# One register value per pair, masked one-hots released pair by pair, QKV two steps per group

## The reference, cut to what matters

```python
h = relu(layernorm(x)); z = ln(h, ln1_g, ln1_b)
q, k, v = (z @ W + b).reshape(512, 8, 64)            # Wq, Wk, Wv
scores = einsum('ehd,ehd->eh', q[src], k[dst]) * scale + edge_bias
p = exp(scores - segment_max(scores, src)[src])
out = segment_sum(p / segment_sum(p, src)[src] * v[dst], src)     # layer 0
# then layers 1 to 3: segment sums over the same edges between dense layers
```

## Time and profile before

| | before |
|---|---|
| three runs | 443.1, 440.94, 443.72 us; median 443.1 us |
| profiled execution | 438.14 us, its span 436.7 us |
| TensorE busy | 391.0 us, 90% |
| VectorE busy | 319.4 us, 73% |
| ScalarE busy | 166.9 us, 38% |
| first to last pair matmul | 28.09 to 141.88 us |

### The profile page before, as it was taken

One profiled execution on the slowest core, in us unless ns is written; L12 is line 12 of the kernel. 1 busy time (PEld: TensorE's weight loads), 2 busy tenths in 40 slices (PEclk: granted clock), 3 DMA queues, 4 the chain that ended last, 5 costly groups with the idle time before them and its releaser, 6 DMA issues.

```text
span 436.7 us, 5306 instructions
## 1 busy us (share of the span) xinstructions
PE 391.0 (90%) x1794; PEld 287.8 (66%) x1794; DVE 319.4 (73%) x664; ACT 166.9 (38%) x275; POOL 2.3 (1%) x14
## 2 busy tenths in 40 slices
PE   2679878779889899999898999999978999999995
PEld 1455444445545678888675878878746878877773
DVE  6788958577683588899696697868885568677436
ACT  1625534454210444235346671335244341124420
POOL 2000000000000000000000000000000000000000
PEclk9999989898899899999998999999989999999989
DMA  8405867684521430004640032320050005000002
GB/s 250 191 2 81 109 99 107 93 117 91 72 54 24 146 121 1 2 2 153 238 187 2 0 102 92 101 93 0 1 194 0 0 0 194 0 3 0 0 2 96
DMA packets 16297, 32.94 MB, mean 75 GB/s; under 512 B 1360, under 2 KB 1488, under 8 KB 16272
## 3 DMA queue, kind: packets, MB, share of 16 engines
q1 hardware_dynamic: 15744, 32.25, 29.2%
q10 hardware_dynamic: 528, 0.36, 0.4%
HBM read 21.07 MB, written 1.05 MB: 51 GB/s over the span
## 4 chain that ended last, share of the span: by engine, by line
PE 60%; DVE 21%; DMA 6%; ACT 5%; issue 4%; SPq 0%; DVEq 0%; ACTq 0%
PE acc L1253 7%; PE bank L1335 6%; DMA big<-z_sb 6%; PE bank L1236 6%; PE acc L1124 4%; PE bank L1124 4%; PE acc L1137 3%; PE acc L1138 3%; PE acc L1306 3%; PE bank L1320 3%; PE bank L1138 3%; PE bank L1137 3%; DVE wide_rounded L713 3%; DVE stats L580 2%; DVE c_rounded L719 2%
## 5 line engine op out<-in xcount | busy, mean ns | idle before, releaser
L1253 PE MATMUL acc<-wide_rounded,c_rounded 128*126 128x512 f32 x200 | 64.1, 465 | 15.4 <-issue 7.4
L1253 PEld LDWEIGHTS acc<-wide_rounded,c_rounded 128*126 128x126 f32 x200 | 37.4, 202 | 43.2 <-issue 37.9
L713 DVE TENSOR_SCALAR wide_rounded<-iota_f,picked 128x512 fp32r<-128x512 f32 x100 | 41.8, 481 | 26.3 <-PE acc L1253 25.0
L427 ACT COPY z_sb<-acc 126x512 f32<-126x512 f32 x37 | 21.7, 586 | 71.6 <-PE acc L1253 40.7
L451 ACT ACTIVATE wide<-wide,low_col 128x512 f32<-128x512 f32 x32 | 21.4, 715 | 32.3 <-DVE low_col L829 32.2
L1335 PEld LDWEIGHTS bank<-v_sb,big 128*128 128x128 f32 x256 | 29.9, 192 | 5.2 <-issue 4.8
L1335 PE MATMUL bank<-v_sb,big 128*128 128x65 f32 x256 | 31.7, 277 | 0.0
L1236 PE MATMUL bank<-t_sb,wslot 128*128 128x512 f32 x64 | 31.6, 620 | 0.0
L549 DVE TENSOR_TENSOR wslot_rounded<-wslot,wide_rounded 128x512 fp32r<-128x512 f32 x24 | 16.2, 687 | 20.9 <-ACT wslot L360 20.9
L719 DVE TENSOR_TENSOR c_rounded<-row_bc,wslot_rounded 128x1008 fp32r<-128x1008 bf16 x25 | 30.0, 1201 | 0.0
L576 DVE TENSOR_TENSOR big_rounded<-big,big_rounded 128x1024 fp32r<-128x1024 f32 x24 | 29.1, 1222 | 0.4
(11 more groups left out here) (292 smaller groups left out, 780.1 us busy)
## 6 DMA issues: line engine op xcount, KB each, us to landing
big<-z_sb SPq DMA_DIRECT2D x33, 252.0 KB
big<-in_w SPq DMA_DIRECT2D x4, 2048.0 KB, 7.9
x_sb<-in_x SPq DMA_DIRECT2D x8, 256.0 KB, 5.1
big<-in_w_3t SPq DMA_DIRECT2D x2, 1024.0 KB, 6.7
row_bc<-in_rows SPq DMA_DIRECT2D x7, 256.0 KB, 6.6
wslot<-in_wq SPq DMA_DIRECT2D x1, 1024.0 KB, 8.3
wslot<-in_wk SPq DMA_DIRECT2D x1, 1024.0 KB, 10.2
wslot<-in_wv SPq DMA_DIRECT2D x1, 1024.0 KB, 12.3
```

Source lines behind the costliest of these rows:

```text
L427: nc.scalar.copy(stage[0:BROWS, b % STAGES, :], a).then_inc(S["staged"], 1)
L713: nc.vector.tensor_scalar(hot_ring[:, u, k, :], iota_f[:, :], picked[:, 0, s0 + k:s0 + k + 1], None, ALU.is_equal)
L1253: last = nc.tensor.matmul(to, st_ring[:, u, 2 * k + a, :, :].rearrange("p w k -> p (w k)"), hot_ring[:, u, k, :], start=False, stop=False, ...
```

## The change

It has four parts. (1) `rows_u` keeps one number per pair, the block's number plus one; the wait uses it as it is, and the bank is its low two bits, so `choices` loads 8 values in place of 16, and block b goes to bank (b+1) mod 4. The matmul and the two small VectorE operations for the bank's number go. (2) The value's range is stated, so no assertion is made for the slice. (3) VectorE waits for each pair of group g-2 ahead of the one-hot that overwrites it, in place of once for the whole group. (4) `qkv_group`: two steps after each group from 3 to 15, then two after every other group from 17 to 23; before, two after odd groups and one after even ones, and four after group 23.

```diff
-ENDS, PICK, BANKS, NEEDS = 130, 200, 300, 400
-SPARE = 1
+ENDS, PICK, NEEDS = 130, 200, 400
...
-        rows_u = sb("rows_u", [1, SLOTS, 2], U16)
+        rows_u = sb("rows_u", [1, SLOTS], U16)
...
-        qkv_group = [g for g, steps in enumerate([7, 4, 3] + [2, 1] * 10 + [4]) for _ in range(steps)]
+        qkv_group = [g for g, steps in enumerate([7, 4, 3] + [2] * 13 + [0, 2, 0, 2, 0, 2, 0] + [2]) for _ in range(steps)]
...
-                a = bank[b % ACC][0:BROWS, :]
+                a = bank[(b + 1) % ACC][0:BROWS, :]
...
-            dve.wait_ge(S["tables"], 4)
-            link(nc.vector.tensor_single_scalar(bank_i[:, :], bank_i[:, :], ACC - 1, ALU.bitwise_and))
-            mark(nc.vector.tensor_scalar(bank_c[:, :], bank_i[:, :], float(N), -float(SPARE * N), ALU.mult, ALU.add))
...
-                nc.vector.tensor_single_scalar(rows_u[:, c, 0], bank[4][0:1, column(BANKS)], float(SPARE * N), ALU.add)
-                nc.vector.tensor_single_scalar(rows_u[:, c, 1], bank[4][0:1, column(NEEDS)], float(NBK + 1),
+                nc.vector.tensor_single_scalar(rows_u[:, c], bank[4][0:1, column(NEEDS)], float(NBK + 1),
                                                ALU.add).then_inc(S["rows_ready"], 1)
...
                 for k in ks:
+                    if freed is not None:
+                        dve.wait_ge(S["pair_mm"], freed + (k + 2))
                     nc.vector.tensor_scalar(hot_ring[:, u, k, :], iota_f[:, :], picked[:, 0, s0 + k:s0 + k + 1], None,
                                             ALU.is_equal)
...
-                dve.wait_ge(S["pair_mm"], (g - RING + 1) * GROUP + 1)
-                build(g, g % RING, g * GROUP)
+                build(g, g % RING, g * GROUP, (g - RING) * GROUP)
...
-                dve.wait_ge(S["pair_mm"], j * GROUP + (FIXED - GROUP + 1))
-                build(NG - 1, 0, FIXED)
+                build(NG - 1, 0, FIXED, j * GROUP + (FIXED - RING * GROUP))
...
-                nc.tensor.matmul(bank[4][0:1, column(BANKS)], bank_c[:, :], slot_hot[:, c], start=True, stop=True)
...
-                    rows_u[0:1, s0:s0 + n, :].rearrange("o s a -> o (s a)"), engines=[mybir.EngineType.PE])
+                    rows_u[0:1, s0:s0 + n], engines=[mybir.EngineType.PE], min_val=1, max_val=NBK + 1,
+                    skip_runtime_bounds_check_because="a block's number plus one, made on the chip from a table")
...
-                    to = acc[0:BROWS, bass.ds(held[2 * k], N)]
-                    pe.wait_ge(S["evacuated"], held[2 * k + 1])
+                    pe.wait_ge(S["evacuated"], held[k])
+                    to = acc[0:BROWS, bass.ds((held[k] & (ACC - 1)) * N, N)]
```

More of the change, by code:

```diff
@@ L105, in gnn_kernel @@
         ends = sb("ends", [NBK, 2])
-        bank_c = sb("bank_c", [NBK, 1])
         need_c = sb("need_c", [NBK, 1])
-        bank_i = sb("bank_i", [NBK, 1], I32)
         ends_row = sb("ends_row", [1, NBK + 3])
@@ L335, in _ @@
                            allow_small_or_imprecise_dtypes=True).then_inc(S["tables"], 2)
-            nc.gpsimd.iota(bank_i[:, :], [[0, 1]], base=0, channel_multiplier=1).then_inc(S["tables"], 1)
             nc.gpsimd.iota(need_c[:, :], [[0, 1]], base=-NBK, channel_multiplier=1,
@@ L708, in slot_columns, with one_hots @@
                 step(base + 3, slot_masks(first), False)
-            def one_hots(u, s0, ks=range(GROUP)):
+            def one_hots(u, s0, ks=range(GROUP), freed=None):
                 for k in ks:
+                    if freed is not None:
+                        dve.wait_ge(S["pair_mm"], freed + (k + 2))
                     nc.vector.tensor_scalar(hot_ring[:, u, k, :], iota_f[:, :], picked[:, 0, s0 + k:s0 + k + 1], None,
@@ L724, in left_sides, with build @@
                         [P, 2 * GROUP, BW, KW]), ALU.mult).then_inc(S["built"], 1)
-            def build(g, u, s0):
-                one_hots(u, s0)
+            def build(g, u, s0, freed=None):
+                one_hots(u, s0, freed=freed)
                 left_sides(u, s0)
@@ L1264, in _ @@
             bias_turned()
-            pe.wait_ge(S["tables"], 7)
+            pe.wait_ge(S["tables"], 6)
             pe.wait_ge(S["lows_ready"], 1)
@@ L1275, in _ @@
             for g in range(NG - 1):
-                pairs(g, g % RING, held[2 * GROUP * (g % 2):2 * GROUP * (g % 2 + 1)])
+                pairs(g, g % RING, held[GROUP * (g % 2):GROUP * (g % 2 + 1)])
                 if g == 0:
```

## The result

The changed kernel takes 422.47 us (median of 4 runs, 420.65 to 423.52) against 442.02 us beside it: **0.956, 95% interval 0.949 to 0.963**. The profiled execution took 420.65 us, its span is 419.1 us; 17.6 us of span are gone.

What follows compares the result with a forecast made beforehand. It took TensorE's sequencer to bound the kernel, with transfers already pacing the first part. Block 28's bank free at 102.7 plus 22.2 put the last pair at 124.9; 443.1 - 17.1 gave 426.0 us, range 418 to 434.

Steps and rivals of the forecast that it cites:

- The transfers set the first part's pace: Pair stage to block 28, about 103 us: transfers already set the pace, 2.35 us a block; faster TensorE gains nothing.
- The load's term: Loads of 8 values in place of 16 on TensorE's sequencer: 2.2 us each, saving 2.3 per period.
- Register work: Per pair on TensorE's sequencer: 0.40 us in place of 0.50, bounds 0.25 and 0.50; eight pairs save 0.8 us.
- The signs: What would show it: loads 1.9 to 2.4 us, last pair at 122 to 128, copies to block 28 awaiting DMA.
- the second rival: Transfers cost more than allowed, or the clock drops in their waits: gain 8 to 12, 431 to 435 us; 14%.
- QKV: From group 17 on, 8 steps left where 13 were: five steps, 4.3 us, move to where transfers set the pace.
- One-hots: VectorE's waits pair by pair ahead of its one-hots: costed at 0 to 1 us in all.
- The sum: Block 28's bank free at about 102.7 us, plus 22.2: last pair ends at 124.9 in place of 141.88.
- The 1.3 us for handing over: Added behind block 28 to the longest of four near-equal chains, 20.9 us, making 22.2.
- The slower one: Mask and product make TensorE's sequencer wait ahead of every pair: decides from 0.79 us per pair, 462 at 1.0; 3%.
- The one with a larger gain: Register work 0.25 us per pair, loads 1.92, transfers 2.1 a block: last pair about 119.5, 418 to 421; 9%.
- The one in which a load's time is not by the value: Loads on TensorE's sequencer stay near 4.4 us; gain from register work and QKV alone, 436 to 440 us; 2%.

Runs made afterwards that it cites:

- e7: The changed kernel with loads of 16 values and two slice assertions per pair, both put back: 438.84 us, 0.990 of the kernel before.
- e9: The kernel before with only the new places of the QKV steps: 438.60 us, 0.997.
- e10: The kernel before with only the one-hots released pair by pair: 440.92 us, 0.999.
- e8: The changed kernel with four stage places in place of three, so four transfers may be in flight: 418.24 us, 0.945 of the kernel before.
- e12: The changed kernel transferring only half the columns of each staged block: last block copied 89.6 us after the first pair matmul, in place of 97.0.
- e11: The kernel before transferring only half the columns of each staged block: pair stage 108.6 us in place of 113.8.
- e3: The changed kernel with the QKV steps where they were before: 425.43 us, 0.966 of the kernel before.
- e4: The changed kernel with VectorE waiting for the whole group ahead of the first one-hot, as before: 422.59 us, 0.960 of the kernel before.
- e2: The changed kernel with each load reading 16 values again, 8 of them used: 425.81 us, 0.965 of the kernel before.
- e6: The changed kernel with each pair's slice asserted twice again: 424.86 us, 0.961 of the kernel before.
- e5: The kernel before with the range of the loaded values stated, so no assertions: 428.08 us, 0.967.

## Why the prediction was right

- **The bound before.** The load was what ended the gaps that the profile put down to ScalarE or to "issue". e7 shows it: with loads and assertions as before and the rest new, gaps and period return. QKV (e9: 0.997, 0.993 to 1.000) and one-hots (e10: 0.999) alone do nothing clear to a kernel that its sequencer bounds.
- **The transfers set the first part's pace.** Block 28 moved by 0.58 us where 0.8 were forecast; e8 and e12 confirm the bound. That they set it *already before* was too strong: there both bounds lay side by side. With half the bytes, e11 gained 5.6 us in that part, of which shorter loads can be 3.2, the larger share. The prediction used this only to say that the first part would not get shorter, and that held.
- **The load's term**: 2.2 us forecast, 2.28 measured.
- **Register work** was mis-sized: 0.40 us per pair forecast, with 0.25 as the lower bound; 0.22 measured. The FUSED_REGOPS of 146 ns was gone, where I had kept one. With 0.22 and the measured loads of 2.53, 2.25, 2.68 and 1.24 us the sequencer's chain is 16.8 us (an estimate) and not the longest: TensorE's own 20.4 us is. Since the sum went by the 20.9 of the sequencer, this cost it 0.5 us. That so large a miss cost so little is owed to a second chain of nearly the same length, not to the register term.
- **The signs.** Most came as named, but one did not: the prediction called its size wrong if copies of blocks 29 to 35 waited for DMA rather than TensorE. Six of the seven did, 9.1 us in all. The size held even so, so the sign was badly chosen. Freed of the sequencer's gaps, TensorE finished these blocks before the transfers made room for them, and they left at 2.34 us a block; the waits did not reach it, as from 106.19 us on it has no gap. This was the second rival's condition (transfers bind in the second part) without its price.
- **QKV**: five steps, 4.3 us, forecast; 4.6 measured (e3).
- **One-hots**: 0 to 1 us forecast, 1.1 measured (e4).
- **The sum**: bank free at 102.7, measured 102.96; the last pair at 124.9, its block copied at 124.65 now. The 1.3 us for handing over were an allowance, and about right: from pair 71 at 103.19 to the end are 21.4 us, 1.0 more than TensorE's 20.4.
- **From trace to median.** By the span the forecast was 17.1 us and 17.6 came. The median lay 3.5 us under the 426.0 forecast, since I kept the 5.0 us by which three runs of the kernel before lay above its profiled execution. Over 19 runs of it the median is 440.75, 2.6 above that execution, and the changed kernel's median is 1.8 above its own. That distance is the largest error of the forecast.
- **The rivals.** The slower one needed 0.79 us per pair; it was 0.22. The one with a larger gain had its register work (0.22, under its 0.25), but neither its loads (2.28 in place of 1.92) nor its transfers (from block 10 to block 28 they went at 2.54 us a block in place of 2.1). The one in which a load's time is not by the value falls by the loads of 2.28 us. **The clock** did fall to the 1.2 GHz level in one place, after the gap of 2.51 us at 61 to 64 us:

```profile
64.00:68.50 4.50, 4.50 (x10) 2.20 (x10) 2.29 (x3) 2.35 (x4) 0.00 (x0) 0.62 0.76 117
```

The row gives the granted clock as 0.62 for the stretch. It lies in the first part, where the transfers cover it; from 103 us to the end of the pairs the clock is 1.00.

## What to carry to other kernels

A sequencer's register work is not in the busy shares: where an engine idles without a plausible releaser, lay its loads and register instructions on the timeline and sum a period. A period is the longest of several sums, so what a cost is worth depends on the kernel in which it is tried. Put back into the changed kernel one at a time, long loads and long register work cost 3.7 and 4.4 us by the traces (e2, e6); taken one at a time out of e7, which has both, they give back 12.4 and 13.1 us. The places of the QKV steps are worth 4.6 us in the changed kernel (e3) and 0.7 in the one before (e9). Ask first which sum is the longest, and then which is next. Name the next bound before the change, as it decides how much of the saving arrives: here the transfers, behind which the first part got no shorter, while TensorE could still run ahead as far as its four banks let it, 71 pairs in place of 64.

## What the runs showed that I had not expected

- Register instructions of 18 to 46 ns cost TensorE's sequencer 0.08 to 0.12 us each from start to start; five and two matmuls to a pair cost 0.49 us (e6), two 0.22.
- The mask alone keeps the assertions out: the changed kernel without a stated range gives the same instructions, so part (2) of the change adds nothing to it (read from the program, not timed). In the kernel before, which has no mask, the stated range is what takes them out (e5).
- A load of 16 values took 4.06 us in the median with half the DMA traffic and 4.44 with all of it (e11 and the kernel before, one profile each).
- Four transfers in flight moved 109 GB/s, three 105, between 40 and 100 us; each took 9.0 us in place of 6.5 (e8).
- The lead that TensorE won behind the transfers, 10.1 us of its work, was more than the gaps that went, 7.1 us.
